# Softmax attention: the inverse of the softmax sums moves from DVE's reciprocal to a power of minus one on GpSimd

## The reference, cut to what matters

```
x = x + tanh(g_xattn[0]) * xattn(layernorm(x), ctx)
# in xattn: 8 heads of 8 channels, 256 queries against 256 keys
scores = einsum('bhtc,bhsc->bhts', rotary(q), rotary(k)) / sqrt(8)
p_attn = softmax(scores, axis=-1)
out    = einsum('bhts,bhsc->bhtc', p_attn, v)
out    = Wo @ out + bo
```

## Time and profile before

| what | us |
|---|---|
| median of three runs | 2686.56 |
| lowest and highest | 2667.9, 2697.57 |
| the profiled execution's own time | 2682.36 |
| its span in the trace | 2680.6 |
| first product `on` (L603) begins | 94.3 |
| last product `on` begins | 656.0 |
| first work of the next stage's weights on ACT | 665.4 |

### The profile page before, as it was taken

How to read it: one execution, slowest core, us unless ns; L and a number is a source line. 1 busy time by engine, 2 the same in 40 slices (tenths; PEclk the granted TensorE clock), 3 DMA queues, 4 the chain that set the end, 5 groups by cost and what they waited for, 6 DMA issues and landing times. The chain is left out here.

```text
span 2680.6 us, 60407 instructions
## 1 busy us (share of the span) xinstructions
PE 2266.7 (85%) x20880; PEld 1718.4 (64%) x20880; DVE 1855.2 (69%) x3965; ACT 1159.6 (43%) x2509; POOL 1103.8 (41%) x1111
## 2 busy tenths in 40 slices
PE   6899999885887689995799998999988698999990
PEld 4555555543766567773577877777767577887770
DVE  4888888872556757765778788788787365445754
ACT  2676667664533223333344444444333263333330
POOL 3454445464153500000454454455477600224626
PEclk9897779865888889997999999999989799999995
DMA  5455555442368431201322323322334472446754
GB/s 118 120 115 129 143 129 135 114 125 87 113 215 252 150 134 41 60 29 40 88 66 75 84 66 78 81 72 73 76 96 116 136 240 79 138 137 184 234 159 144
DMA packets 249859, 313.10 MB, mean 117 GB/s; under 512 B 45152, under 2 KB 202848, under 8 KB 249056
## 3 DMA queue, kind: packets, MB, share of 16 engines
q1 hardware_dynamic: 188592, 219.11, 29.3%
q0 software_dynamic: 26624, 58.79, 8.0%
q10 hardware_dynamic: 34352, 31.34, 3.5%
HBM read 122.40 MB, written 102.24 MB: 84 GB/s over the span
## 5 line engine op out<-in xcount | busy, mean ns | idle before, releaser
L2084 POOL TENSOR_TENSOR ca_qk<-ca_qk,ca_q_swap 128x512 f32<-128x512 f32 x160 | 249.3, 1558 | 366.5 <-DVE ca_q_swap L2262 366.2
L731 DVE TENSOR_REDUCE soft_top<-soft_pa 128x2 fp32r<-128x512 f32 x512 | 328.1, 683 | 101.2 <-PE soft_pa L811 98.1
L626 ACT ACTIVATE soft_prob<-soft_pb 128x512 f32<-128x512 f32 x512 | 285.7, 594 | 190.4 <-PE soft_pb L804 187.9
L804 PE MATMUL soft_pb<-soft_rep 25*128 25x256 f32 x1024 | 210.2, 378 | 46.5 <-DVE soft_top L731 27.0
L804 PEld LDWEIGHTS soft_pb<-soft_rep 25*128 25x128 f32 x1024 | 137.3, 225 | 169.6 <-issue 85.3
L1416 PE MATMUL moe_pgu<-moe_w_hi,moe_xt_hi 128*128 x472 | 196.1, 415 | 38.9 <-DVE moe_xt_lo L1333 30.1
L811 PE MATMUL soft_pa<-soft_rep 24*128 24x256 f32 x1024 | 219.2, 384 | 5.8 <-DVE soft_top L731 3.5
L1435 PE MATMUL moe_py<-moe_w_d,moe_at 128*128 x788 | 217.8, 392 | 1.5 <-issue 0.8
L1338 DVE TENSOR_TENSOR moe_act_f<-moe_silu,moe_pgu 128x256 f32<-128x256 f32 (+1 forms) x236 | 88.4, 375 | 151.0 <-ACT moe_silu L1253 150.4
L2353 PE MATMUL ca_py<-ca_w_hi,ca_ot_hi 128*128 128x256 f32 x512 | 157.6, 308 | 35.0 <-DVE ca_ot_lo L2283 34.8
L1253 ACT ACTIVATE moe_silu<-moe_pgu 128x256 f32<-128x256 f32 (+1 forms) x236 | 82.1, 348 | 230.6 <-PE moe_pgu L1416 230.3
(11 more groups left out here) (377 smaller groups left out, 6376.3 us busy)
## 6 DMA issues: line engine op xcount, KB each, us to landing
ca_q_swap<-ca_q_f SPq DMA_DIRECT2D x640, 64.0 KB
moe_xs<-moe_rows SPq DMA_DIRECT2D x236, 128.0 KB, 2.1
soft_rep<-soft_parts SPq DMA_DIRECT2D x378, 64.0 KB
moe_rows<-soft_blank SPq DMA_DIRECT2D x27, 768.0 KB, 3.7
moe_ys_rows<-moe_ys ACTq DMA_DIRECT2D x134, 128.0 KB, 1.7
moe_ys<-moe_ys ACTq DMA_DIRECT2D x102, 128.0 KB, 2.3
moe_xd<-scratch SPq DMA_DIRECT2D x64, 128.0 KB, 2.6
ca_vs<-ca_v SPq DMA_DIRECT2D x32, 256.0 KB, 3.7
```

Source lines behind the costliest of these rows:

```text
L626: act.activation(prob[:, k % 4, h, :], p_b[:, 2 * T * h:2 * T * (h + 1)], ACT.Exp).then_inc(prob_ready, 1)
L731: dve.tensor_reduce(heads[:, j, :, g], p_a[:, 2 * T * h:2 * T * (h + 1)].rearrange("p (c s) -> p c s", c=HALF), AX, ALU.max).then_inc(a_do ...
L804: mm = pe.matmul(p_b[:, out], rep[of, i % 4, g, at:at + PART], rep[of, i % 4, g, 0:T], start=True, stop=True)
L2084: pool.tensor_tensor(qk[:, u % 2, m, :], qk[:, u % 2, m, :], q_swap[:, p % 2, :], ALU.add).then_inc(qk_ready, 1)
```

## The change: what it does

DVE's reciprocal at the end of each iteration goes, with its wait for the DMAs of `packed` and `sums`. POOL takes over that wait and computes `rsum` itself, as `sums` to the power of `minus_one`, a column of -1 that is broadcast over the 256 positions. It does so just ahead of the product `on`. The wait for `rsum` between the two stays; it is now a wait of POOL for its own result. One memset at the start fills `minus_one`.

```diff
-        half_neg = sb("half_neg", [PART, 1])
+        half_neg, minus_one = sb("half_neg", [PART, 1]), sb("minus_one", [PART, 1])
...
-                pool.wait_ge(zeroed, 5)
+                pool.memset(minus_one[:], -1.0).then_inc(zeroed, 1)
+                pool.wait_ge(zeroed, 6)
...
                     if live(t):
+                        pool.wait_ge(pack_in[t % 2], PACK * (t // 2 + 1))
+                        past(pool, on_ready, t)
+                        pool.tensor_tensor(rsum[:], sums[:, t % 2, :], minus_one[:].to_broadcast([PART, T]), ALU.pow).then_inc(rsum_ready, 1)
                         pool.wait_ge(rsum_ready, t + 1)
                         past(pool, wo_ready, t - 1)
                         pool.tensor_tensor(on[:, t % 2, :], packed[:, t % 2, :], rsum[:], ALU.mult).then_inc(on_ready, 1)
...
-                    t = i - 1
-                    if live(t):
-                        dve.wait_ge(pack_in[t % 2], PACK * (t // 2 + 1))
-                        past(dve, on_ready, t)
-                        dve.reciprocal(rsum[:], sums[:, t % 2, :]).then_inc(rsum_ready, 1)
```

## The result

The changed kernel takes 3807.57 us (median of four runs, 3806.8 to 3807.76) against 2685.8 us before (median of four). The ratio is 1.418, with a 95% interval of 1.411 to 1.426. The forecast was 3810 us. The profiled execution of the changed kernel took 3806.8 us, 1124 us more than that of the kernel before.

The account below looks back on a forecast made before the run. PE and DVE alternating set the first stage's pace; POOL would take over. First power to 134.6, plus 1333.8, 235.5, sends 41.2 and held iterations 38.4 gives 1783.5 us, +1126.8, so 3810 us; range 3640 to 3960.

Parts of the forecast that it names:

- first power begins: Start of the first stage: the first power starts at 94.3 us, where the first product began in the earlier trace.
- eight times four sends: Eight first-stage iterations carry four sends behind the product, now in line on POOL: 8 x 5.15 = 41.2 us.
- rest of the last five iterations: Iterations 28 to 32, without rstd, roped or parts: DMA landing uncovered at 1.6 us, 47.1 us each including the power.
- The price of the power: New POOL instruction: 153 ns a column from one- and four-column powers, so 39.6 us at 256 columns.
- Both bends of the line: Rivals on the power's price: 20.1 us giving 3186 us (chance 0.08), or 64.5 us giving 4607 us (chance 0.03).
- POOL sets the stage: First stage: POOL's iteration becomes 51.3 us instead of 18.1, with PE, DVE and ACT work fitting under the power.
- The break-even of 6.4 us: First stage: a power under 6.4 us, or 23 ns a column, would leave POOL's iteration within 18.1 us.
- The rest of POOL's iteration: POOL's ordinary iteration without the power: 11.7 us, with the remainder beginning 9.5 us after xo, behind ACT's half.
- DVE held by POOL: Six iterations with choose, place or weigh: two-input DVE operations stand until the power ends, 57.7 us each, 38 us in all.
- The removed reciprocals: End of DVE's first-stage iterations: 32 x 1.744 = 55.8 us removed, worth nothing once POOL sets the pace.
- the rival with a cheap power: First stage: power costs 1.2 us like the product and fits POOL's slack, kernel faster at 2664 us; chance 0.07.

Follow-up runs that it names:

- the run without the power: Changed kernel with POOL's power replaced by one product with a small constant, so outputs are undivided: 2674.0 us, 0.9963 of the kernel before.
- the three narrower kernels: Changed kernel with the power over only 128, 64 or 32 of 256 columns, the rest left undivided: 3152.7, 2822.2 and 2698.9 us.

## Why the prediction was right, point by point

The forecast was 3810 us and the measured time 3807.6. That close a hit is in part luck: the powers came out 50 us longer, the rest of the iterations 22 us and the held iterations 38 us shorter, and these nearly cancel. Up to the end of the last product the sum is 2.6 us short, and the stages behind took 4.9 us less. The table is for the profiled execution up to the end of the last product. The measured rest of POOL's iterations is what remains between the starts of the first power and of the 27th, 1367.3 us, without 26 powers and 3 times the sends.

| term of the sum | forecast us | measured us |
|---|---|---|
| first power begins | 94.3 | 101.8 |
| 32 powers | 32 x 39.6 = 1267 | 32 x 41.15 = 1317 |
| rest of 26 iterations | 26 x 11.7 = 304 | 282 |
| DVE held in six iterations | 38 | 0 |
| eight times four sends | 41.2 | 8 x 5.2 = 41.4 |
| rest of the last five iterations | 38 | 43 |
| end of the last product | 1783.5 | 1786.1 |

**The price of the power** was right in kind. Two narrow widths gave 153 ns a column, four wider ones give 159.4. The line through 32 to 256 columns leaves 5.443 - 32 x 0.1594 = 0.34 us for an empty instruction, and one column measured 0.55, so the first few columns do not lie on it. The 4% came from there and not from the exponent, as the run with -0.5 shows. Both bends of the line are excluded by the three widths. The factor of two that the Trainium skill's "GPSIMD Engine Reference" gives for elementwise work (section on engine selection) does not cover a power: 41.15 us against DVE's 1.74 is a factor of 24.

**POOL sets the stage** was right. The other engines' work fitted under the power. The break-even of 6.4 us is where the straight line from the wider powers points (6.2), but the kernel is slower than the one before already at 5.44 us.

**The rest of POOL's iteration** was forecast at 11.7 us and is 10.1 in the shortest iterations (starts of the power 51.28 apart). The step that was off is the wait for ACT's half. I took 8.0 us from `low` to the remainder out of the earlier trace rows. In the changed kernel it is 6.9 us, and the remainder begins 8.1 us after `xo`, not 9.5. ACT's half now begins when POOL's own `roped` ends, and only ACT's 0.6 us stands in front of the remainder. In the kernel before PE still had a block of scores to make after `low`, ahead of `maxima(i, 5)`; here it was made under the power. The other way goes a wait that the sum put at nothing in these 26 iterations: POOL stood before the power for the landing of `packed` and `sums` in 14 of them, 13.5 us in all. In the last five, where the sum had 1.6 us each for it, it was 1.8 to 3.4 us.

**DVE held by POOL** failed as a term: 38 us forecast, none measured. The mechanism is seen beside POOL's sums and differences. At the end of iteration 21 of the changed kernel `picked`, DVE's two-input operation, takes 0.96 us beside the remainder. First DVE, then POOL, in order of time:

```profile
1137.31 0.96 DVE L237 TENSOR_TENSOR soft_r_picked<-soft_r_left,soft_r_score 128x32 f32<-128x32 f32 x1
```

```profile
1136.96 1.27 POOL L599 TENSOR_TENSOR soft_parts<-soft_roped,soft_parts 128x512 fp32r<-128x512 f32 x1 [0.74 <-ACT soft_parts L688]
1138.66 41.15 POOL L604 TENSOR_TENSOR soft_rsum<-soft_sums,soft_minus_one 128x256 f32<-128x256 f32 x1 [0.43 <-DMA soft_sums<-soft_o_raw]
```

It ended at 1138.27, with POOL's difference at 1138.23, and before the power began. Two things were wrong in the term. `choose` was through before the power, and a power of 256 columns holds DVE's two-input operations only until some 0.48 us behind its start: later ones take 0.15 us for one column and 0.42 us for 256. The step drew from the held `low` beside a sum that any instruction of POOL holds DVE to its own end. The rule in the key points of the Trainium skill's "GPSIMD Engine Reference" (contention with instructions of two SBUF inputs) names the pair of engines rightly; how much it costs depends on what POOL does, and for the power the runs show at most half a microsecond. Nor is it a matter of arithmetic alone: `shift` (L173), one column with two inputs, takes 1.07 to 1.08 us in 12 of its 16 times in the changed kernel, while POOL only issues DMAs. In the other four it takes 0.15 us, beside such issues too; what makes the difference is not shown.

```profile
354.11 1.07 DVE L173 SCALAR_TENSOR_TENSOR soft_r_shift<-soft_r_mv,soft_r_rstd 128x1 f32<-128x1 f32 x1
```

**The removed reciprocals** were worth nothing in the changed kernel, as forecast. For the rival with a cheap power I had given them half of 45 us; the run without the power measured about 10.

**What stays open.** The first power began 7.5 us later than in my sum, and in the three narrower kernels it began between 96.6 and 99.6; why the start of the stage moves is not shown. Two iterations of the changed kernel, those that end with the powers at 1195.7 and 1248.9 us, lasted 57.1 and 53.2 us. They come near the 57.7 us forecast for held iterations but are no such case. In the first PE's 30 router matmuls stood ahead of ACT's half for 6.41 us. In the second PE and ACT waited for DVE's `place`, whose two-input operations were through before its power. Why the removal of 1.74 us on DVE gives back only 0.3 us an iteration is argued from PE's 89% in the run without the power, not shown.

## What to carry to other kernels

The same function costs differently on each engine by more than the usual factor: before a step is moved to an engine that looks idle, find the slope of that very operation in the trace, from two widths of it, and multiply it out to the new width. Then compare it with the slack of the receiving engine's iteration, not with its busy share: well below the slack it is nearly free, near it a part shows (16 us in all for the power of 5.44 us), above it every microsecond counts once an iteration. And a contention seen beside one kind of instruction is to be measured beside the other kind, at its start and in its middle, before it becomes a term.

## What the runs showed of the hardware that was not expected

- A power on GpSimd costs 159.4 ns a column from 32 to 256 columns on 128 partitions, for the exponents -1 and -0.5 alike; the product at the same width took 0.61 to 0.73 us.
- Behind the first half microsecond of a 41 us power VectorE's operations with two SBUF inputs keep their time (0.15 us for one column, 0.42 us for 256). One of 256 columns that begins in the first 0.43 us ends 0.89 to 0.90 us behind the start of the power, whenever it began. Beside a GpSimd sum or difference of 512 columns such operations end with it (1.40 us and 0.96 us).
- A VectorE product of 128 columns with two SBUF inputs, begun within 0.1 us behind the start of a power, ends 0.39, 0.44, 0.55 and 0.76 us behind it with powers of 32, 64, 128 and 256 columns. The time for which it is held grows by some 1.7 ns a column (an estimate from these four), the power itself by 159.4.
- While GpSimd only issues DMAs, a VectorE operation of one column with two SBUF inputs took 1.07 us in 12 of 16 cases and 0.15 us in four.
- A product with a broadcast column took 0.61 us, one with a full second input 0.73 us, both 256 columns wide.
- `Ln` and `Exp`, one behind the other on ScalarE, loaded a table each, 1.28 us a load.
- The runs of the changed kernel spread by 1.0 us, those of the kernel before by 29.7. The stage in which PE and DVE alternate seems to be where the kernel before spreads; no run tests that.
